# Top-k attention of a decoder kernel: selected probabilities as a difference of two exponentials, sums from the 32 top values, keys one batch element further ahead, loads split in two

## The reference, cut to what matters

```python
# x_text (16, 112, 256), x_vision (16, 375, 192), H = 4 heads of DH = 32
Q = (x_text @ Wq).reshape(Bb, Tt, H, DH)
K = (x_vision @ Wk).reshape(Bb, Gg, H, DH)
scores = jnp.einsum('bthd,bghd->bhtg', Q, K) / np.sqrt(DH).astype(np.float32)
scores = jnp.where(vision_mask[:, None, None, :], scores, -jnp.inf)
topv, topi = jax.lax.top_k(scores, K_TOP)            # K_TOP = 32
probs = jax.nn.softmax(topv, axis=-1)
attn = jnp.zeros_like(scores).at[bi, hi, ti, topi].set(probs)
attn_mean = attn.mean(axis=1)                         # over the 4 heads
V = x_vision @ Wv
c_t = jnp.einsum('btg,bgd->btd', attn_mean, V) * text_mask[..., None]
```

## Time and profile before

| | us |
|---|---|
| median of 3 runs | 2929.61 |
| lowest, highest | 2921.18, 2934.15 |
| profiled execution | 2931.85 |
| its span in the trace | 2929.9 |
| PE busy, share of the span | 2318.0, 79% |
| DVE busy | 1627.6, 56% |
| POOL busy | 736.4, 25% |
| ACT busy | 687.3, 23% |

### The profile page before, as it was taken

How to read it: one execution, slowest core, us unless ns; L and a number is a source line. 1 busy time by engine, 2 the same in 40 slices (tenths; PEclk the granted TensorE clock), 3 DMA queues, 4 the chain that set the end, 5 groups by cost and what they waited for, 6 DMA issues and landing times.

```text
span 2929.9 us, 36786 instructions
## 1 busy us (share of the span) xinstructions
PE 2318.0 (79%) x14932; PEld 1592.5 (54%) x14932; DVE 1627.6 (56%) x3160; ACT 687.3 (23%) x1321; POOL 736.4 (25%) x667
## 2 busy tenths in 40 slices
PE   4444589999987999799999999886576767985776
PEld 1111245555555666688888887775354442953432
DVE  5888744444443333355565556663788876035335
ACT  3222132232221111222322222221222210011122
POOL 1222279505020000444434343431100003001000
PEclk8666798898886999899999999997666657578888
DMA  2000010000001000100100101000401000500000
GB/s 82 0 0 0 19 66 9 9 13 9 9 8 44 1 1 0 69 1 1 57 1 1 57 1 43 1 1 1 114 24 31 25 16 0 132 1 0 0 0 25
DMA packets 49703, 64.12 MB, mean 22 GB/s; under 512 B 30856, under 2 KB 46976, under 8 KB 48384
## 3 DMA queue, kind: packets, MB, share of 16 engines
q1 hardware_dynamic: 49536, 61.78, 6.9%
HBM read 59.71 MB, written 2.06 MB: 21 GB/s over the span
## 4 chain that ended last, share of the span: by engine, by line
PE 69%; DVE 19%; DMA 4%; POOL 3%; ACT 3%; issue 2%; SPq 1%; POOLq 0%; DVEq 0%; ACTq 0%
PE PS L1192 7%; PE PS L1208 7%; DVE st_h L470 4%; PE PS L609 4%; PE PS L949 4%; PE PS L1772 3%; PE PS L928 3%; PE PS L1109 3%; DMA ctx_k<-in_ctx 3%; PE PS L1709 3%; DVE st_h L479 2%; PE PS L635 2%; PE PS L1804 2%; PE PS L620 2%; PE PS L648 2%
## 5 line engine op out<-in xcount | busy, mean ns | idle before, releaser
L271 POOL TENSOR_SCALAR ln_ve<-ln_mv 128x2 f32<-128x2 f32 (+1 forms) x95 | 21.1, 222 | 1699.6 <-DVE ln_mv L255 1699.5
L325 PE MATMUL PS<-bc_parts,ident 96*128 96x448 bf16 x256 | 87.9, 436 | 160.1 <-DVE st_h L479 150.3
L1384 DVE TENSOR_TENSOR p_x<-PS,cols 128x1024 f32<-128x1024 f32 x112 | 129.3, 1217 | 147.7 <-PE PS L1154 147.6
L1446 POOL TENSOR_TENSOR q_x<-q_f,cols 128x2048 f32<-128x2048 f32 x56 | 208.6, 3744 | 9.8 <-ACT q_f L1304 9.8
L792 DVE TENSOR_REDUCE XD<-PS 112x2 f32<-112x750 f32 x128 | 120.3, 940 | 127.5 <-PE PS L635 127.4
L635 PE MATMUL PS<-k_s,q_s 32*112 32x375 f32 x512 | 128.2, 557 | 41.6 <-DVE XD L792 40.8
L761 ACT ACTIVATE e_t<-PS 125x672 f32<-125x672 f32 x128 | 93.5, 730 | 253.3 <-PE PS L648 253.2
L325 PEld LDWEIGHTS PS<-bc_parts,ident 96*128 96x128 bf16 x256 | 22.2, 107 | 235.7 <-DVE st_h L479 193.1
L1013 DVE SCALAR_TENSOR_TENSOR XA<-PS,gate_w,XA 112x256 f32<-112x256 f32 x128 | 61.9, 484 | 135.4 <-PE PS L949 135.4
L522 POOL TENSOR_TENSOR st_h<-st_h 128x448 f32<-128x448 f32 x64 | 71.9, 1135 | 249.2 <-DVE st_h L479 248.8
L648 PE MATMUL PS<-q_s,k_s 32*125 32x112 f32 x1536 | 126.7, 298 | 1.1 <-ACT e_t L761 1.1
(11 more groups left out here) (328 smaller groups left out, 5152.7 us busy)
## 6 DMA issues: line engine op xcount, KB each, us to landing
t_ring<-k_scratch SPq DMA_DIRECT2D x16, 784.0 KB, 4.9
enc_w<-in_enc_w SPq DMA_DIRECT2D x2, 3072.0 KB, 10.1
wc<-in_enc_w SPq DMA_DIRECT2D x2, 3072.0 KB, 12.0
ctx_k<-in_ctx SPq DMA_DIRECT2D x16, 281.2 KB
wc<-in_wc SPq DMA_DIRECT2D x1, 4096.0 KB, 13.9
enc_rows<-in_enc_rows SPq DMA_DIRECT2D x4, 896.0 KB, 12.4
ctx_t<-in_ctxT SPq DMA_DIRECT2D x16, 187.5 KB, 2.4
ctx_f<-in_ctxT SPq DMA_DIRECT2D x16, 187.5 KB
```

The source lines that it names most:

```text
L325: last = pe.matmul(ps[2 * (j % 2) + m][:, 0:QT], ident16[0:96, s:s + 1].to_broadcast([96, P]), bc_parts[0:96, q * QT:(q + 1) * QT], start= ...
L1384: last = dve.tensor_tensor(p_x[:, m, :, :, :], ps[1][:, m * P:(m + 1) * P].rearrange("p (h i) -> p h i", i=16).unsqueeze(2) .to_broadcast( ...
L1446: last = pool.tensor_tensor(q_x[:, c, :, :].rearrange("p t (h i) -> p t h i", i=16), q_f[:, k % 2, c, :].rearrange("p (t i) -> p t i", i=1 ...
```

## The change

- A second exponential (ACT, `exp_rest`, L1887 of the changed kernel): after the fourth turn of a head, exp(`w_s` - maximum) goes to a new tile `e_r` (the trace's names call it `wc`, in which it lies; `w_s` lies in `wb`, now with a slot for each head). Fillers give zero, so the difference `e_p` - `e_r` keeps the selected entries and zeroes the others.
- The difference (POOL, one `tensor_tensor` of 112 x 375 per head) is written over `e_p`. DVE's masking instruction L1936 is gone.
- The sum (ACT): an exponential of the head's 32 top values, 112 x 32, accumulates `e_sum`. `top8` has a slot per head for that.
- On DVE the weights of b-1 are worked out behind the first pair of b. On ACT `spread` of b-1 (the matrices `dg`) stands behind `exp_rest` of heads 0 and 1 of b.
- Keys are made two batch elements ahead: PE runs scores(b+1), keys(b+2), context(b).
- Loads are split: `ctx_f` of b+1 is issued ahead of `ctx_k` of b, on a semaphore of its own, once keys(b-1) are done; keys wait for the two `ctx_f` loads, L1733 (the old L1717) for `ctx_k`.

```diff
+            features(0)
             for b in range(B):
+                if b + 1 < B:
+                    features(b + 1)
                 if b >= 2:
                     sp.wait_ge(m_ready, m_count("m1", b - 2) + 1)
...
             def keys(b):
                 bank = m_claim(pe, "k", b)
-                pe.wait_ge(ectx_loaded[b % 2], 48 * (b // 2 + 1))
+                pe.wait_ge(ctx_loaded[b % 2], 32 * (B // 2 + b // 2 + 1))
...
                 bank = m_claim(pe, "at", b)
                 pe.wait_ge(x_dg, b + 1)
+                pe.wait_ge(x_masked, MASKED_0 + XH * (b + 1))
...
+            keys(1)
             for b in range(B):
                 if b + 1 < B:
-                    keys(b + 1)
                     scores(b + 1)
+                if b + 2 < B:
+                    keys(b + 2)
                 context(b)
...
+            def exp_rest(b, h):
+                n = XH * b + h
+                act.wait_ge(x_cut, CUT_0 + n + 1)
+                if n >= 2:
+                    act.wait_ge(x_masked, MASKED_0 + n - 1)
+                    act.wait_ge(x_total, SUM_0 + 2 * (n - 1))
+                act.activation(e_r[:, n % 2, :], w_s[:, h, :], ACT.Exp, bias=neg_m[:, h:h + 1]).then_inc(x_total, 1)
+                act.activation(e_top[:, n % 2, :], top8[:, h, :, :].rearrange("t k j -> t (k j)"), ACT.Exp,
+                               bias=neg_m[:, h:h + 1], accum_out=e_sum[:, b % 2, h:h + 1]).then_inc(x_total, 1)
...
+            for b in range(B):
+                exp_all(b, 0)
+                exp_all(b, 1)
+                if b + 1 < B and b >= 1:
+                    copy_keys(b + 1)
+                exp_rest(b, 0)
+                exp_rest(b, 1)
+                if b >= 1:
+                    spread(b - 1)
+                exp_all(b, 2)
+                exp_all(b, 3)
+                if b >= 1:
+                    copy_attention(b - 1)
+                    copy_context(b - 1)
+                exp_rest(b, 2)
+                exp_rest(b, 3)
...
-                        last = link.mark(dve.scalar_tensor_tensor(e, w_s[:, a, :], FILL, e, ALU.is_equal, ALU.mult,
-                                                                  accum_out=e_sum[:, b % 2, h:h + 1]))
...
+                    if b >= 1 and h0 == 0:
+                        weights(b - 1)
...
+            for n in range(B * XH):
+                b, h = divmod(n, XH)
+                e = e_p[:, XH * (b % 2) + h, :]
+                pool.wait_ge(x_exp, n + 1)
+                pool.wait_ge(x_total, SUM_0 + 2 * n + 1)
+                pool.tensor_tensor(e, e, e_r[:, n % 2, :], ALU.subtract).then_inc(x_masked, 1)
```

More of the change, by code:

```diff
@@ L147, in build @@
         k_e = sb("k_e", [P, 2, S2], pool=s4a)
-        w_s = sb("w_s", [T, 2, S2], pool=s4a)
         e_p = sb("e_p", [T, 2 * XH, S2], pool=s4a)
-        top8 = sb("top8", [T, 2, 4, 8], pool=s4a)
+        top8 = sb("top8", [T, XH, 4, 8], pool=s4a)
+        e_top = sb("e_top", [T, 2, 32], pool=s4a)
         neg_m = sb("neg_m", [T, 4], pool=s4a)
@@ L167, in build @@
         s4x.close()
+        flat_b = wb[:, :, :].rearrange("p k d -> p (k d)")
+        w_s = flat_b[0:T, 0:XH * S2].rearrange("t (h s) -> t h s", h=XH)
+        e_r = wc[0:T, 7168:7168 + 2 * S2].rearrange("t (z s) -> t z s", z=2)
         m1 = XD
@@ L1599, in build @@
             "g_done f2x_ready f2x_added").split())
+        x_cut, CUT_0 = max_done, PAIRS
+        x_total, SUM_0 = exp_done, PAIRS
+        x_masked, MASKED_0 = pair_added, 8 * len(UNITS)
         S4_ROWS = ("g_in", "b_in", "bf_in", "bf_out", "g_ffn", "b_ffn", "b2", "g_out", "b_out")
@@ L1628, in s4x_load, with features @@
                 .then_inc(em_loaded, 16)
+            def features(b):
+                if b >= 2:
+                    sp.wait_ge(m_ready, m_count("k", b - 2) + 1)
+                for i in range(2):
+                    sp.dma_start(ctx_f[0:CR[i], b % 2, i, :], dr["ctxT"][b, i * P:i * P + CR[i], :])\
+                        .then_inc(ctx_loaded[b % 2], 16)
+            features(0)
             for b in range(B):
+                if b + 1 < B:
+                    features(b + 1)
                 if b >= 2:
                     sp.wait_ge(m_ready, m_count("m1", b - 2) + 1)
-                for i in range(2):
-                    sp.dma_start(ctx_f[0:CR[i], b % 2, i, :], dr["ctxT"][b, i * P:i * P + CR[i], :])\
-                        .then_inc(ectx_loaded[b % 2], 16)
                 sp.dma_start(ctx_k[:, b % 2, :, :], dr["ctx"][b].rearrange("(j p) f -> p j f", p=JR))\
@@ L1647, in m_uses @@
         def m_uses():
-            uses = [("q", q) for q in range(NQ)] + [("k", 0)]
+            uses = [("q", q) for q in range(NQ)] + [("k", 0), ("k", 1)]
             for b in range(B):
-                if b + 1 < B:
-                    uses.append(("k", b + 1))
+                if b + 2 < B:
+                    uses.append(("k", b + 2))
                 uses += [("at", b), ("m1", b)]
@@ L1714, in context @@
                 pe.wait_ge(m_used, m_count("at", b) + 1)
+                pe.wait_ge(ectx_loaded[b % 2], 16 * (b // 2 + 1))
                 for i in range(2):
@@ L1853, in copy_context, with exp_all, spread @@
                             .then_inc(m_used, 1)
[L1855 to L1869, removed]
+            def exp_all(b, h):
+                n = XH * b + h
+                act.wait_ge(x_first, n + 1)
+                if b >= 2 and h == 0:
+                    act.wait_ge(m_ready, m_count("at", b - 2) + 1)
+                act.activation(e_p[:, XH * (b % 2) + h, :], ps[h][0:T, 0:S2], ACT.Exp,
+                               bias=neg_m[:, h:h + 1]).then_inc(x_exp, 1)
+            def exp_rest(b, h):
+                n = XH * b + h
+                act.wait_ge(x_cut, CUT_0 + n + 1)
[5 more added lines that the diff above has]
+                               bias=neg_m[:, h:h + 1], accum_out=e_sum[:, b % 2, h:h + 1]).then_inc(x_total, 1)
+            def spread(b):
                 act.wait_ge(x_rs, b + 1)
@@ L1874, in s4x_act @@
                 last.then_inc(x_dg, 1)
+            copy_keys(0)
+            copy_keys(1)
+            for b in range(B):
[14 more added lines that the diff above has]
+                exp_rest(b, 3)
+            spread(B - 1)
             copy_attention(B - 1)
@@ L1901, in s4x_dve, with weights @@
             dve.wait_ge(xa_copied, B // 2)
+            def weights(b):
+                dve.wait_ge(x_total, SUM_0 + 2 * XH * (b + 1))
+                link(dve.reciprocal(e_rs[:, b % 2, :], e_sum[:, b % 2, :]))
+                dve.tensor_scalar(e_rs[:, b % 2, :], e_rs[:, b % 2, :], tmk[:, b:b + 1], 1.0 / XH,
+                                  ALU.mult, ALU.mult).then_inc(x_rs, 1)
             for b in range(B):
@@ L1915, in s4x_dve @@
                                 link.after(cut[a])
-                            s = ps[h][0:T, 0:S2] if turn == 0 else w_s[:, a, :]
-                            found[a] = link.mark(dve.max(top8[:, a, turn, :], s))
+                            s = ps[h][0:T, 0:S2] if turn == 0 else w_s[:, h, :]
+                            if turn == 0 and b >= 1:
+                                dve.wait_ge(x_total, SUM_0 + 2 * (n - 3))
+                            found[a] = link.mark(dve.max(top8[:, h, turn, :], s))
                         if turn == 0:
@@ L1920, in s4x_dve @@
                                 link.after(found[a])
-                                found[a] = link.mark(dve.tensor_scalar(neg_m[:, h:h + 1], top8[:, a, 0, 0:1], -1.0,
+                                found[a] = link.mark(dve.tensor_scalar(neg_m[:, h:h + 1], top8[:, h, 0, 0:1], -1.0,
                                                                        None, ALU.mult))
@@ L1924, in s4x_dve @@
                             link.after(found[a])
-                            s = ps[h][0:T, 0:S2] if turn == 0 else w_s[:, a, :]
-                            ins = dve.match_replace(w_s[:, a, :], top8[:, a, turn, :], s, FILL)
+                            s = ps[h][0:T, 0:S2] if turn == 0 else w_s[:, h, :]
+                            ins = dve.match_replace(w_s[:, h, :], top8[:, h, turn, :], s, FILL)
                             if turn == 0:
                                 ins.then_inc(x_first, 1)
+                            elif turn == 3:
+                                ins.then_inc(x_cut, 1)
                             else:
                                 cut[a] = link.mark(ins)
[L1932 to L1935, removed]
-                        last = link.mark(dve.scalar_tensor_tensor(e, w_s[:, a, :], FILL, e, ALU.is_equal, ALU.mult,
-                                                                  accum_out=e_sum[:, b % 2, h:h + 1]))
[L1938 to L1941, removed]
+                    if b >= 1 and h0 == 0:
+                        weights(b - 1)
+            weights(B - 1)
             dve.wait_ge(m_used, len(M_AT))
```

## The result

| | before | changed |
|---|---|---|
| median of 11 runs each | 2928.88 us | 2942.9 us |
| lowest, highest | 2921.18, 2934.15 | 2936.38, 2952.92 |
| ratio, 95% interval | | 1.0055 (1.0041 to 1.0069) |
| span of the profiled execution | 2929.9 | 2938.9 |
| DVE's first max to the last context product | 338.6 | 355.7 |

The change makes the kernel slower by about half a percent, 14 us. The forecast was 2946.3 us, range 2918 to 2968.

A forecast was written before the change was run, and what follows sets the result against it. Bound by the load-keys-scores-context chain, replaced by a dg loop: 16.1 + 14 x 21.5 + 3 x 6.2 + 22.7 = 358.4 against 338.6, less 3.1 at the start, +16.7: 2946.3 us, range 2918 to 2968.

The forecast's parts named there:

- The loop: DVE pair 0, ACT exponentials and dg, PE context product, L1733, scores, DVE again: a new loop as long as the old.
- The turn: One pass of the new loop without values: 21.5 us, between 20.5 and 22.4, with TensorE's clock taken halfway.
- First max to context product: DVE's first max of b to context(b-1) on PE, through pair 0, exponentials and dg: 10.6 us.
- the sign: What would show the forecast right: DVE idles 4 to 6 us per turn before a max, released by PE.
- The small exponential: ACT's exponential of 32 values with a sum: taken as 0.3 us, between nothing and 0.52 plus an accumulator read, 0.6.
- the rival in which POOL holds DVE: POOL's differences slow DVE in pair 0 of each turn: +24 us on the forecast, 2970 us; chance 7%.
- scores to max: Last step of the turn, from scores on PE to DVE's max: 2.9 us in both low and high sums.
- my low end: Lower bound of the turn's length, from the short context product and L1717 times: 20.5 us.
- values: Values between L1717 and scores, no longer covered by the load: 6.2 us each for b = 3, 7 and 11, between 4.6 and 7.8.
- Start and end: First keys no longer wait for the third load, 3.1 us saved; last context starts 22.7 us into DVE's last batch element.
- The most likely outcome named: Whole kernel measurably slower than before, above 2944 us: chance 58%.
- the line of 2944: Upper edge of what a measurement cannot tell from no change, about 0.5% or 14.6 us; above it counts as slower.

The follow-up runs named there:

- the two experiments on the place of dg: Weights and dg moved early in the changed kernel: 2878.6 us; moved late in the kernel with keys ahead, loads split and old masking (2888.1 us): 2927.8 us.
- three moves: Changed kernel with weights and dg early, values behind the next scores, ACT's context copy ahead of exponentials of heads 2 and 3: 2852.4 us, ratio 0.9766.
- The kernel with keys ahead: Kernel before with only keys a batch element further ahead and loads split, masking and sum still on DVE: 2888.1 us, ratio 0.9855.
- the late place: Keys two ahead, loads split, DVE's old masking, plus weights and dg of b-1 moved behind pair 0 of b: 2927.8 us, ratio 1.0002 to before.

## Why the prediction was right

**The loop.** Its one decision, that dg behind pair 0 closes a loop over DVE, ACT and PE as long as the one it opens, held step by step, and the two experiments on the place of dg show it as cause: 64 us one way, 40 the other. The chain has the members that were named, no DMA in it, and PE never waits for POOL.

**The turn.** Forecast 21.5 us, between 20.5 and 22.4; measured 18.9 to 22.1, mean 20.8 over the eleven turns of the loop without values. Seven of them lie within those bounds, and DVE waits 4.9 to 5.8 us in them; four lie below, at 18.9 to 19.3, with waits of 2.5 to 2.9 where 4 to 6 was the sign. First max to context product: 2239.50 - 2229.00 = 10.5, forecast 10.6. The pieces on ACT (two of each, the small one in two records) and DVE beside POOL:

```profile
L1976 DVE MATCH_REPLACE8 wb<-top,wb 112x375 f32<-112x375 f32 x163 | 85.7, 534 | 0.0
L1967 DVE MAX8 top<-wb 112x8 f32<-112x375 f32 x162 | 80.3, 538 | 0.0
...
L2073 POOL TENSOR_TENSOR e_p<-e_p,wc 112x375 f32<-112x375 f32 x54 | 48.0, 909 | 260.0 <-ACT wc L1887 260.0
...
L1888 ACT ACTIVATE e_top<-top,neg_m 112x32 f32<-112x32 f32 x54 | 16.7, 309 | 0.0
...
L1888 ACT ACTIVATION_READ_ACCUMULATOR e_top<-top,neg_m 112x1 f32 x54 | 10.2, 190 | 0.0
```

The small exponential takes 0.31 with a read of 0.19 that overlaps it; both together advance ACT by the 0.3 taken, and both ends of its range fell away. POOL's difference is 0.91 where 0.86 was scaled, and is hidden. Max and replace last 538 and 534 ns, as before: the rival in which POOL holds DVE, 2970 us, is out, as the two max in the earlier trace rows had hinted.

**A size that was off: scores to max.** The sum had 2.9 at either clock. It is 2.8 at the low one and 1.5 at the high one. The turn 2210.56 to 2229.47, at the high clock from its context product on, is the short kind:

```profile
2210.56 0.54 DVE top L1967
...
2220.59 4.76 PE PS L1724 x24
2225.91 1.61 PE PS L1733 x12
2227.52 0.85 PE PS L1712 x8
...
2229.47 0.54 DVE top L1967
```

18.9, below my low end of 20.5. I took the 2.9 from one place of the kernel before, where the granted clock was 0.50, and did not ask what the clock would do to it.

**A size that was off: values.** Forecast 6.2 each, in a range of 4.6 to 7.8; all three took 7.2 and 0.6, the dearer end. The price at the high clock, estimated at 4.0, stood in the trace of the kernel before, where the three in the loop took 3.83 and only the fourth 7.20:

```profile
2157.90 3.83 PE L1726 MATMUL PS<-XD,enc_w 128*128 128x448 f32 x8 [0.58 <-ACT XD L1848]
```

The clock in three stretches of the changed kernel (last context product of a turn at 2240, values at 2249, scores of a short turn at 2226):

```profile
2240.00:2245.00 5.00, 4.85 (x24) 4.58 (x22) 5.00 (x18) 0.43 (x2) 0.00 (x0) 0.50 0.00 0
2249.00:2256.00 7.00, 7.00 (x8) 1.87 (x8) 0.00 (x0) 0.53 (x1) 0.00 (x0) 0.50 0.29 82
2226.00:2229.00 3.00, 3.00 (x29) 2.00 (x29) 0.45 (x2) 1.44 (x6) 0.40 (x1) 1.00 0.04 8
```

The turns came in a fixed pattern of four, and the one with values was at 0.50 each time. I had treated the clock as a coin for each turn; it repeated with the turns.

**Start and end.** 4.9 us were saved at the start, not 3.1: the wait of 3.29 in the earlier trace rows went whole, and scores came at the high clock behind it. The last product starts 21.5 after the last batch element's first max, forecast 22.7.

**Together.** Stage 355.7 against a forecast of 358.4; with the start +12.3 net in the traces against +16.7, and 14 us in the medians. The errors in the stage are -0.2 for the first batch element, -0.7 x 11 = -7.9 for the turns without values, +2.2 x 3 = +6.6 for those with values (29.9 against 21.5 + 6.2), and -1.2 at the end; the start adds -1.8. The loop and its members were right by reasoning. That the sum came within 3 us of the stage was partly luck: two errors of 7 to 8 us, both from the clock, nearly cancel. The most likely outcome named, slower than the line of 2944, was missed by 1 us, though the interval of the ratio, 1.0041 to 1.0069, excludes no change.

## What to carry to other kernels

Taking work off the busiest engine shortens nothing while that engine is not in the chain: before one moves an instruction, one writes down the loop that its new place closes, through every engine's program order, and compares its length with the loop that is opened. Here the work that mattered, four copies that take 1.2 us together, was no new work at all; put behind two exponentials that wait for DVE's fourth turn, it made PE wait for a whole pair of DVE. A change of several parts should be run part by part: -40 and +130 us alone, +14 together, and -71 (against the kernel before on the same chip) once three moves are made.

## What the runs showed of the hardware

- TensorE's clock came with the pattern of the loop: turns with the same work took 18.9, 21.3 or 22.1 us, in a fixed order that repeated every four turns (18.8 to 19.0 and 22.1 in alternation once values were moved). In the kernel before the context product from 2407.38 on was followed by 16 us of nearly unbroken matmuls at 0.50, while the first one, also behind an idle PE, was at 1.00 within 4 us.
- What decides between the two is not shown, and a busier TensorE is not the answer by itself. The kernel with keys ahead had PE busy 230 of 298 us at a mean granted clock of 0.62; the same matmuls with the late place were busy 176 of 337 us at 0.68:

```profile
2072.10:2409.60 337.50, 176.19 (x865) 126.11 (x865) 292.75 (x992) 75.63 (x194) 5.45 (x6) 0.68 0.17 43
```

- 96 matmuls that nobody reads went with a kernel 14 us faster and a granted clock of the stage up from 0.63 to 0.78.
- The eight instructions of values took 3.83 to 3.86 us where the granted clock was 1.00 and 7.20 us where it was 0.50.
- The unchanged stages ahead took 2049.66 us in one execution and 2058.26 in another, up to their last copy; a difference of spans has to be split by stage before a few us are given to a change.
